# Gate tiles moved from the input projection into the scan, and a dt stage of its own, in a one-core decoder layer

## Chip, cores and metric

One core of one Trainium2 chip runs the whole layer as one program. The time is the device time of one execution in microseconds (us), as a median of runs: 3565.0 us over three runs, 3561.2 to 3567.3.

## The reference, cut to what matters

The layer is a selective scan block, a cross attention and a gated feed-forward, each followed by a layer norm. The change touches the first block, and the control flow of the second.

```
proj = hidden @ in_proj_w                  # 1024 x 1024 tokens by 1024 x 4096
x, z = split(proj)                         # x: 16 tiles of 128 channels, z: 16 gate tiles
xc = silu(conv4(x) + conv_b)
ssm = xc @ x_proj                          # 96 rows: 64 of dt, 16 of B, 16 of C
dt_r, Bm, Cm = rmsnorm of the three parts
dt = softplus(dt_r @ dt_proj + dt_bias)    # 16 tiles of 128 channels
scan over 512 steps, 16 states a channel:  h = exp(dt A) h + dt B xc ;  ys = C h
y = (ys + D * xc) * silu(z)
out = y @ out_proj                         # then residual and layer norm
```

Weights and activations are float32. The large products are made of three passes over pairs (high part, rest), at one pass a matmul; a product written directly on float32 operands shows as two matmul records.

## The kernel before, in words

Five phases run one after the other: `mamba_in`, `mamba_scan`, `project_norm_qkv`, `attention`, `attention_out_feed_forward`. A phase begins when every engine has ended the one before. Within a phase each engine has its own program in a fixed order, and semaphores tie them together; nothing is scheduled at run time.

`mamba_in` makes 32 tiles `main(m, s)` of 128 channels by 1024 tokens, each 8 x 2 x 3 = 48 matmuls (L95 to L97). Tiles 0 to 15 are x: VectorE convolves, ScalarE applies silu, and `xproj` adds the tile's share of the 96 rows. Tiles 16 to 31 are the gate z: ScalarE evicts each with Silu (L264) and SyncE stores it to `sz`. Once the 96 rows are whole, ScalarE and VectorE make their rms norm (L289 to L374), and the dt stage begins. It runs between the gate tiles, two dt tiles at a time: TensorE multiplies (L470), ScalarE makes |v|, relu(v), exp(-|v|) and ln(1 + exp) (L302, L303, L306, L311), VectorE a correction term and the sums (L382, L385, L389, L392), GpSimd the product u = dt * xc (L422; the last two are VectorE's, L406), and dt and u go to DRAM. xc stays in SBUF for the scan.

`mamba_scan` has 32 iterations (16 tiles of 128 channels, 2 batches) of 8 pairs of states. A pair n passes GpSimd (`dbx`, L725), ScalarE (exp into PSUM, L676), VectorE (the scan, L699, then the product with C, L688; for two pairs in eight the scan writes `g` itself and GpSimd multiplies, L713), and TensorE, which sums it over partitions. TensorE's program goes by t, two pairs each, 128 in all: at every fourth t the D term (L761), then `wait_product` and the four sums of t (L766), then two matmuls of the key projection of the context (`key_product`, L748). The pairs pass through four buffers `g`; pair n takes its buffer when the sums of pair n - 4 are done.

`project_norm_qkv` begins with 32 steps of the output projection. In each, SyncE loads y, the gate and the weights, GpSimd multiplies y by the gate (L1208), ScalarE and VectorE split into high part and rest, and TensorE multiplies. `attention` runs 32 heads in a loop of four rounds with eight heads each (`heads`, L1343).

Of the kernel before, what the change touches and what calls it, by code (L numbers as in the profile page):

```python
# [31 lines left out]
E = R + 2 * NS  # L32
CTX = 1024
# [66 lines left out]
def mamba_in(nc, res, d, xc):  # L100
# [21 lines left out]
    under = Arena(nc, "in_under", sb.at)  # L122
# [14 lines left out]
    dtw = [sb(f"dtw{s}", [R, P]) for s in range(2)]
    dt_b = sb("dt_b", [P, IT])

    ssm, sq, rms, ssm_n = acc[0][0:E], acc[1][0:E], pre[0][0:E], pre[1][0:E]  # L140
    rl, ee = ([over(f"{n}{s}", [P, B, L]) for s in range(2)] for n in ("rl", "ee"))
    dd, ll = acc, [pre[0], sb("ll", [P, B, L])]
# [8 lines left out]
    sz_st = [sem(f"sz_st{s}") for s in range(2)]  # L151
# [19 lines left out]
    sz, dt, u = (d[n].rearrange("(b i) p l -> i p b l", b=B) for n in ("sz", "dt", "u"))  # L171

    with nc.Block() as block:
        @block.sync
        def _(sp):
# [20 lines left out]
            sp.dma_start(dt_b[:], d["dt_bias"]).then_inc(par_ld, 16)  # L196
            for s in range(2):
                sp.dma_start(dtw[s][:], d["dt_w"][s]).then_inc(dtw_ld[s], 16)
            with sp.Fori(0, IT // 2) as j:
                for s in range(2):  # L200
                    next_w(2 * j + s, s)
            for s in range(2):
                next_w(IT + s, s)
                store_gate(IT + s, s)

            def store_dt(i, s):
                sp.wait_ge(dt_done, i + 1)
                sp.dma_start(dt[i], dd[s][:]).then_inc(dt_st[s], 16)

            def store_u(i, s):  # L210
                sp.wait_ge(u_done, i + 1)
                sp.dma_start(u[i], uu[s][:]).then_inc(u_st[s], 16)

            with sp.Fori(IT // 2 + 1, IT - 1) as j:
                next_w(2 * j, 0)
                store_gate(2 * j, 0)
                next_w(2 * j + 1, 1)
                i = 2 * j - IT - 2
                for s in range(2):
                    sp.wait_ge(dt_mm, i + s + 1)  # L220
                    sp.dma_start(dtw[s][:], d["dt_w"][i + s + 2]).then_inc(dtw_ld[s], 16)
                store_gate(2 * j + 1, 1)
                for s in range(2):
                    store_dt(i + s, s)
                for s in range(2):
                    store_u(i + s, s)
# [1903 lines left out]
```

## Time and profile before

| | |
|---|---|
| median of the runs | 3565.0 us (3561.2 to 3567.3) |
| the profiled execution | 3563.01 us, its span 3561.7 us |
| mamba_in, to the scan's first instruction | 0 to 432 us |
| mamba_scan, to its last store | 432 to 1235 us |
| project_norm_qkv | 1240 to about 1710 us |
| attention | about 1710 to 2405 us |
| busy over the span: TensorE, VectorE, ScalarE, GpSimd | 85%, 61%, 43%, 39% |

The shares are means over stages that have different limits: TensorE is at 9 tenths everywhere but in the scan, where VectorE is. Clock columns give the granted TensorE clock as a share of full speed; 0.50 is 1.2 GHz and 1.00 is 2.4 GHz. The durations of matmuls overlap, since matmuls are pipelined: the pace is read from their starts.

### The profile page before, as it was taken

How to read it: one execution, taken by the hardware profiler on the slowest of the kernel's cores; microseconds unless marked ns; L12 is line 12 of the kernel's file. 1: busy time of each engine (PE TensorE's matmuls, PEld its weight loads, DVE VectorE, ACT ScalarE, POOL GpSimd, SP SyncE). 2: the span in 40 equal slices, each digit the busy share in tenths (PEclk: the TensorE clock that was granted, in tenths of full speed). 3: DMA queues.
4: the chain of work that ended last, by engine and by line, in shares of the span. 5: the costliest groups of instructions: out<-in, count | busy, mean ns of one | idle time of the engine just before them, and what ended most of it. 6: DMA issues, size and time to landing. Idle time of an engine off the chain costs nothing. (4 is left out here: it accounts for less than half of the span.)

```text
span 3561.7 us, 39589 instructions
## 1 busy us (share of the span) xinstructions
PE 3035.0 (85%) x12955; PEld 2247.7 (63%) x12955; DVE 2181.1 (61%) x1669; ACT 1537.8 (43%) x2404; POOL 1395.1 (39%) x794
## 2 busy tenths in 40 slices
PE   9999745555555499999799999998799999999996
PEld 7877511111111178888587878776678888888884
DVE  6554489999999855701477777775644334324426
ACT  4457644554454432411387888772231121111111
POOL 0002299999999722000387878770100000000001
PEclk9999866666666699999899999998999999999998
DMA  3124474454454276312111111115311111111101
GB/s 111 41 77 168 165 180 109 112 118 109 113 119 110 73 281 205 128 66 92 63 37 32 31 36 31 31 33 200 94 52 45 44 56 53 35 53 53 47 18 59
DMA packets 150381, 310.04 MB, mean 87 GB/s; under 512 B 27488, under 2 KB 40544, under 8 KB 148864
## 3 DMA queue, kind: packets, MB, share of 16 engines
q1 hardware_dynamic: 132704, 299.13, 28.3%
q10 hardware_dynamic: 17568, 9.66, 0.9%
q8 instruction: 43, 0.70, 0.1%
q14 instruction: 66, 0.54, 0.1%
HBM read 244.45 MB, written 64.29 MB: 87 GB/s over the span
## 5 line engine op out<-in xcount | busy, mean ns | idle before, releaser
L725 POOL TENSOR_TENSOR scan_dbx<-scan_u,scan_b_bc 128x1024 f32<-128x1024 f32 x256 | 594.3, 2357 | 37.8 <-DMA scan_u<-u 37.8
L1512 POOL TENSOR_TENSOR at_p_lo<-at_p,at_p_hi 128x512 fp32r<-128x512 f32 x384 | 516.6, 1352 | 163.0 <-ACT at_p_hi L1418 152.8
L766 PE MATMUL scan_ps_y<-scan_g,scan_sel 128*32 128x512 f32 x1024 | 212.8, 914 | 355.1 <-DVE scan_g L688 330.9
L676 ACT ACTIVATE scan_ps_a<-scan_dt,scan_a_neg 128x512 f32<-128x512 f32 (+1 forms) x512 | 332.0, 680 | 380.4 <-DVE scan_g L688 365.2
L887 POOL TENSOR_TENSOR ff_y<-ff_y,ff_rstd 128x512 f32<-128x512 f32 x14 | 24.9, 1807 | 1123.3 <-DVE ff_rstd L876 1123.3
L699 DVE TENSOR_TENSOR_SCAN scan_ps_a<-scan_ps_a,scan_dbx 128x1024 f32<-128x1024 f32 x192 | 432.3, 2282 | 0.0
L1457 DVE TENSOR_REDUCE at_neg_max<-at_ps_mx 128x1 fp32r<-128x1536 f32 x132 | 232.0, 1758 | 168.8 <-PE at_ps_mx L1532 157.1
L766 PEld LDWEIGHTS scan_ps_y<-scan_g,scan_sel 128*32 128x32 f32 x1024 | 27.9, 129 | 473.0 <-DVE scan_g L688 291.6
L1415 ACT ACTIVATE at_p<-at_ps_s 128x512 f32<-128x512 f32 x384 | 227.8, 593 | 108.0 <-PE at_ps_s L1549 90.0
L1932 DVE TENSOR_TENSOR ff_hf<-ff_sg,ff_ps_u 128x1024 f32<-128x1024 f32 x28 | 34.2, 1221 | 388.3 <-PE ff_ps_u L97 388.3
L1418 ACT ACTIVATE at_p_hi<-at_p 128x512 fp32r<-128x512 f32 x384 | 242.8, 632 | 12.3
L688 DVE TENSOR_TENSOR scan_g<-scan_ps_a,scan_c_bc 128x1024 f32<-128x1024 f32 x192 | 230.4, 1200 | 0.3 <-PE scan_ps_y L766 0.3
L95 PE MATMUL in_ps<-in_x_hi,in_w_hi 128*128 128x512 f32 x512 | 202.5, 396 | 0.0
L96 PE MATMUL in_ps<-in_x_lo,in_w_hi 128*128 128x512 f32 x512 | 201.2, 393 | 0.0
L97 PE MATMUL in_ps<-in_x_hi,in_w_lo 128*128 128x512 f32 x512 | 200.7, 392 | 0.0
L748 PEld LDWEIGHTS scan_ps_x<-scan_cx,scan_wk 128*128 128x128 f32 x384 | 101.2, 291 | 155.2 <-issue 140.8
L95 PE MATMUL ff_ps_g<-ff_x_hi,ff_w_hi 128*128 128x512 f32 x448 | 176.2, 393 | 5.7 <-DVE ff_x_lo L1872 5.7
L748 PE MATMUL scan_ps_x<-scan_cx,scan_wk 128*128 128x256 f32 x384 | 174.0, 600 | 7.6 <-DMA scan_cx<-in_ctx 7.6
L96 PE MATMUL ff_ps_g<-ff_x_lo,ff_w_hi 128*128 128x512 f32 x448 | 175.2, 391 | 0.0
L97 PE MATMUL ff_ps_g<-ff_x_hi,ff_w_lo 128*128 128x512 f32 x448 | 174.9, 390 | 0.0
L95 PE MATMUL ff_ps_u<-ff_x_hi,ff_w_hi 128*128 128x512 f32 x448 | 174.7, 390 | 0.0
L97 PE MATMUL ff_ps_u<-ff_x_hi,ff_w_lo 128*128 128x512 f32 x448 | 174.3, 389 | 0.0
(254 smaller groups left out, 7429.6 us busy)
## 6 DMA issues: line engine op xcount, KB each, us to landing
scan_dt<-dt SPq DMA_DIRECT2D x128, 256.0 KB, 4.6
scan_u<-u SPq DMA_DIRECT2D x128, 256.0 KB, 7.6
ff_w<-in_w SPq DMA_DIRECT2D x56, 512.0 KB, 4.3
in_w<-in_w_in SPq DMA_DIRECT2D x32, 512.0 KB, 3.7
mid_w<-in_w_out SPq DMA_DIRECT2D x32, 512.0 KB, 5.0
ff_w<-in_w SPq DMA_DIRECT2D x56, 256.0 KB, 2.6
ff_wo_wo<-in_w_o SPq DMA_DIRECT2D x32, 384.0 KB, 3.0
sz<-in_xz SPq DMA_DIRECT2D x16, 512.0 KB, 3.0
```

The costliest lines, as they stand in the source:

```text
L95: nc.tensor.matmul(out, w_hi, x_hi, start=start, stop=False)
L96: nc.tensor.matmul(out, w_hi, x_lo, start=False, stop=False)
L97: return nc.tensor.matmul(out, w_lo, x_hi, start=False, stop=stop)
L676: nc.scalar.activation(at[:, h * L + h:(h + 1) * L], dt[it % 2][:, c, h:L], ACT.Exp, scale=a_neg[:, it % IT, e:e + 1]).then_inc(a_ready, 1)
L688: nc.vector.tensor_tensor(g[n % SG][:].rearrange("p (h l) -> p h l", h=2), ps_a[n % SA][:].rearrange("p (h l) -> p h l", h=2), c_bc[:, n / ...
L699: nc.vector.tensor_tensor_scan(out[:], ps_a[n % SA][:], dbx[n % SL][:], 0.0, ALU.mult, ALU.add).then_inc(scanned, 1)
L725: nc.gpsimd.tensor_tensor(dbx[n % SL][:].rearrange("p (h l) -> p h l", h=2), u[it % 2][:, c:c + 2], b_bc[:, b, k // 2].unsqueeze(1).to_bro ...
L748: last = nc.tensor.matmul(ps_x[:, 0:TOKS], wk[:, k, i * P:(i + 1) * P], cx[:, k], start=k == 0, stop=k == HT - 1)
L766: nc.tensor.matmul(ps_y[c * CW:(c + 1) * CW], sel[:], g[(2 * t + c // 2) % SG][:, h * L:(h + 1) * L], start=False, stop=m == NB - 1).then_ ...
L1418: nc.scalar.activation(p_hi[t % NSL][:], p[t % NSL][:], ACT.Copy).then_inc(p_hi_done, 1)
L1457: nc.vector.tensor_reduce(neg_max[:, i, HD:HD + 1], ps_mx[:].rearrange("p n l -> p (n l)"), AX_X, ALU.max, negate=True).then_inc(max_done, 1)
L1512: nc.gpsimd.tensor_tensor(p_lo[t % NSL][:], p[t % NSL][:], f32(p_hi[t % NSL][:]), ALU.subtract).then_inc(p_lo_done, 1)
```

## The change

Of the 16 gate tiles, `mamba_in` keeps two. The other 14 (`ZN`) are computed in the scan phase by TensorE, as plain float32 products, one tile and batch a unit of eight matmuls, in two halves of four. `UNITS` says at which of the 16 values of t in a block they stand; there are eight blocks, seven of them with four gate units each. The key projection goes the same way, a unit of eight matmuls at one t. For it the scan phase loads x, the weights `wz` and, since SBUF has no room left for xc, one tile of xc an iteration; `mamba_in` stores xc to DRAM. The gate is stored without silu, and the output projection applies it on ScalarE.

The dt stage now follows the last tile of `mamba_in`. It has four buffers each for exp, ln and dt, three PSUM slots for the product, a fourth PSUM tile for the correction term, no relu on ScalarE (VectorE takes the maximum with 0 and adds ln in one instruction), and dt_bias as a 65th row of the product. The loop of four rounds in `attention` is written out.

```diff
+ZN = IT - 2
 def mamba_in(nc, res, d):
-    NT = 2 * IT
+    NT = 2 * IT - ZN
+    ps_x, ps_t = [ps_dt[0], ps_dt[1], ps[0]], ps[1]
 # SyncE
+            def store_conv(m):
+                sp.wait_ge(xc_done, m + 1)
+                sp.dma_start(xc_out[m], xc4[:, :, m, :]).then_inc(xc_st, 16)
...
 # ScalarE
+            def exponentials(i):
+                act.wait_ge(dt_mm, i + 1)
+                if i >= ND:
+                    act.wait_ge(c_done, i - ND + 1)
+                nc.scalar.activation(ee[i % ND][:], ps_x[i % 3][:], ACT.Abs).then_inc(abs_done, 1)
+                act.wait_ge(abs_done, i + 1)
+                nc.scalar.activation(ee[i % ND][:], ee[i % ND][:], ACT.Exp, scale=-1.0).then_inc(e_done, 1)
+            def logarithm(i):
...
+            for i in range(0, IT, 2):
+                exponentials(i)
+                exponentials(i + 1)
+                logarithm(i)
+                logarithm(i + 1)
 # VectorE
+            for i in range(IT):
+                dve.wait_ge(e_done, i + 1)
+                dve.wait_ge(dt_done, i)
+                nc.vector.tensor_scalar(ps_t[:], ee[i % ND][:], 1.0, -1.0, ALU.add, ALU.add).then_inc(t_done, 1)
+                dve.wait_ge(l_done, i + 1)
...
+                nc.vector.scalar_tensor_tensor(dd[i % ND][:], ps_x[i % 3][:], 0.0, ll[i % ND][:],
+                                               ALU.max, ALU.add).then_inc(r_done, 1)
+                dve.wait_ge(t_done, i + 1)
+                nc.vector.tensor_tensor(ps_t[:], ee[i % ND][:], ps_t[:], ALU.subtract).then_inc(c_done, 1)
+                dve.wait_ge(c_done, i + 1)
+                dve.wait_ge(r_done, i + 1)
+                nc.vector.tensor_tensor(dd[i % ND][:], dd[i % ND][:], ps_t[:], ALU.add).then_inc(dt_done, 1)
 # TensorE
+            main(IT + 1, 1, mean_squares)          # the norm's two products stand in the middle of tile 17
+            def dt_product(i):
+                if i >= 3:
+                    pe.wait_ge(r_done, i - 2)
...
 def mamba_scan(nc, res, d):
-    KPB = 2
+    UNITS = {at: (kind, i) for i_at, (kind, i) in (
+        ((0, 2), ("z", 0)), ((2, 4), ("z", 1)), ((4, 5), ("k", 0)), ((6, 7), ("k", 1)),
+        ((8, 10), ("z", 2)), ((10, 12), ("z", 3)), ((12, 13), ("k", 2))) for at in range(*i_at)}
+    ENDS = {"z": (1, 3, 9, 11), "k": (4, 6, 12)}
...
+            def copy_gate(q):
+                m, b = divmod(q, B)
+                act.wait_ge(z_mm, q + 1)
+                act.wait_ge(z_st[b], 16 * m)
+                nc.scalar.activation(zb[b][:], ps_x[:], ACT.Copy).then_inc(zb_done, 1)
...
+            def gate_unit(q, half):
+                m, b = divmod(q, B)
+                if half == 0:
+                    pe.wait_ge(x_ld, 16 * HT)
+                    pe.wait_ge(wz_ld[m % ZC], 16 * (m // ZC + 1))
+                    free_x("z", q)
+                for k in range(HT // 2 * half, HT // 2 * (half + 1)):
+                    last = nc.tensor.matmul(ps_x[:], wz[m % ZC][:, k], x[:, k, b * L:(b + 1) * L], start=k == 0, stop=k == HT - 1)
...
 def project_norm_qkv(nc, res, d):
             def step(n, s):
+                act.wait_ge(a_ld[s], 32 * (n // 2 + 1))
+                nc.scalar.activation(gate[s][:], gate[s][:], ACT.Silu).then_inc(silu_done, 1)
                 act.wait_ge(used, n)
...
-                    pool.wait_ge(a_ld[s], 32 * (j + 1))
+                    pool.wait_ge(silu_done, 2 * j + s + 1)
 def attention(nc, res, d):
-        with eng.Fori(0, NW // 2) as j:
-            for s in range(2):
-                for g in range(G):
-                    body(2 * G * j + G * s + g, 2 * j + s, g, s)
+        for w in range(NW):
+            for g in range(G):
+                body(G * w + g, w, g, w % 2)
```

In VectorE's program of `mamba_in`, two dt tiles before read as follows (`over_ee` is exp, `pre` and `ll` are ln, `over_rl` is relu, `acc` is dt).

```order
L382 TENSOR_SCALAR in_acc_61<-in_over_ee_87 128x1024
L382 TENSOR_SCALAR in_acc_62<-in_over_ee_88 128x1024
L385 TENSOR_TENSOR in_acc_61<-in_over_ee_87,in_acc_61 128x1024
L385 TENSOR_TENSOR in_acc_62<-in_over_ee_88,in_acc_62 128x1024
L389 TENSOR_TENSOR in_acc_61<-in_acc_61,in_pre_63 128x1024
L389 TENSOR_TENSOR in_acc_62<-in_acc_62,in_ll 128x1024
L392 TENSOR_TENSOR in_acc_61<-in_acc_61,in_over_rl_85 128x1024
L392 TENSOR_TENSOR in_acc_62<-in_acc_62,in_over_rl_86 128x1024
```

Now two dt tiles of VectorE are these (`in_ps` is the PSUM tile of the correction term, `in_ps_dt` the product).

```order
L349 TENSOR_SCALAR in_ps<-in_tail_ee_81 128x1024
L354 SCALAR_TENSOR_TENSOR in_tail_dd_89<-in_ps_dt,in_tail_ll_85 128x1024
L357 TENSOR_TENSOR in_ps<-in_tail_ee_81,in_ps 128x1024
L360 TENSOR_TENSOR in_tail_dd_89<-in_tail_dd_89,in_ps 128x1024
L349 TENSOR_SCALAR in_ps<-in_tail_ee_82 128x1024
L354 SCALAR_TENSOR_TENSOR in_tail_dd_90<-in_ps_dt,in_tail_ll_86 128x1024
L357 TENSOR_TENSOR in_ps<-in_tail_ee_82,in_ps 128x1024
L360 TENSOR_TENSOR in_tail_dd_90<-in_tail_dd_90,in_ps 128x1024
```

It is four instructions a tile in both, but one tile after the other in place of two interleaved, and each has at most one SBUF operand beside a PSUM one.

TensorE's program in the scan, from its start, was this (`scan_g` are the pairs, `scan_ps_x` the key projection).

```order
L761 MATMUL scan_ps_y<-xc,scan_d_diag_1466 32x512 x4
L766 MATMUL scan_ps_y<-scan_g_1455,scan_sel 32x512 x2
L766 MATMUL scan_ps_y<-scan_g_1456,scan_sel 32x512 x2
L748 MATMUL scan_ps_x<-scan_cx,scan_wk 128x256 x2
L766 MATMUL scan_ps_y<-scan_g_1457,scan_sel 32x512 x2
L766 MATMUL scan_ps_y<-scan_g_1458,scan_sel 32x512 x2
L748 MATMUL scan_ps_x<-scan_cx,scan_wk 128x256 x2
```

It is now this.

```order
L786 MATMUL scan_ps_y<-scan_xs_1334,scan_d_diag_1328 32x512 x4
L792 MATMUL scan_ps_y<-scan_g_1317,scan_sel 32x512 x2
L792 MATMUL scan_ps_y<-scan_g_1318,scan_sel 32x512 x2
L772 MATMUL scan_ps_x<-scan_x,scan_wz_1337 128x512 x4
L792 MATMUL scan_ps_y<-scan_g_1319,scan_sel 32x512 x2
L792 MATMUL scan_ps_y<-scan_g_1320,scan_sel 32x512 x2
L772 MATMUL scan_ps_x<-scan_x,scan_wz_1337 128x512 x4
```

Four matmuls of 512 columns stand where two of 256 did, and the first of them, at t = 0, needs all of `scan_x`.

SyncE's issues at the start of the scan phase went, after u of iteration 1, straight to the key weights (`scan_wk`) and the context.

```order
L577 DMA scan_c_bc<-bc 32x2048 x4
L571 DMA scan_dt_1448<-dt 32x4x512 x4
L571 DMA scan_u_1450<-u 32x4x512 x4
L598 DMA scan_wk<-in_w_k 128x3072
L590 DMA scan_cx<-in_ctx 128x8x256
```

Ten loads of 512 KB (x and the first two `wz`) and two of 256 KB (xc) now come before them.

```order
L548 DMA scan_c_bc<-bc 32x2048 x4
L561 DMA scan_xs_1334<-xc 128x512
L542 DMA scan_dt_1310<-dt 32x4x512 x4
L542 DMA scan_u_1312<-u 32x4x512 x4
L561 DMA scan_xs_1335<-xc 128x512
L583 DMA scan_x<-in_x_t 128x1024 x8
L564 DMA scan_wz_1337<-in_w_in 128x1024
L564 DMA scan_wz_1338<-in_w_in 128x1024
L586 DMA scan_wk<-in_w_k 128x3072
L572 DMA scan_cx<-in_ctx 128x8x256
```

## Rows read from the trace of the kernel before

**Rows 1.** Busy tenths in 40 slices of the span (the page).
```profile
PE   9999745555555499999799999998799999999996
DVE  6554489999999855701477777775644334324426
```
**Rows 2.** Two stretches: length, busy us (count) by engine, clock, DMA share, GB/s.
```profile
218.00:420.00 202.00, 200.32 (x794) 148.97 (x793) 93.19 (x77) 143.88 (x133) 43.97 (x14) 0.98 0.42 148
463.00:1232.00 769.00, 425.31 (x1648) 134.90 (x1648) 767.32 (x444) 380.97 (x841) 730.64 (x315) 0.66 0.48 113
```
**Rows 3.** Order of time in mamba_in: start, us, engine, line, operation, idle before.
```profile
218.52 1.03 ACT L264 ACTIVATE in_xz<-in_ps 128x1024 f32<-128x1024 f32 x1 [2.69 <-PE in_ps L97]
219.91 1.02 ACT L289 ACTIVATE in_acc<-in_ps_dt 96x1024 f32<-96x1024 f32 x1 [0.35 <-PE in_ps_dt L97]
418.00 0.39 PE L95 MATMUL in_ps<-in_x_hi,in_w_hi 128*128 128x512 f32 x1
419.37 0.39 PE L95 MATMUL in_ps<-in_x_hi,in_w_hi 128*128 128x512 f32 x1
427.40 1.25 SPq L242 DMA_DIRECT2D bc<-in_pre  x1
432.22 0.41 ACTq L648 DMA_DIRECT2D scan_a_exp<-in_a_log  x1
```
**Rows 4.** Groups of instructions in 0 to 450 us: busy us, mean ns.
```profile
L470 PE MATMUL in_ps_dt<-in_pre,in_dtw 64*128 64x512 f32 x64 | 30.5, 618 | 1.7 <-DMA in_dtw<-in_dt_w 1.7
L372 DVE RECIPROCAL in_acc<-in_pre 96x1024 f32<-96x1024 f32 x1 | 6.5, 6550 | 9.8 <-ACT in_pre L294 9.8
L363 DVE SCALAR_TENSOR_TENSOR in_pre<-in_xz,in_cw,in_acc 128x1024 f32<-128x1024 f32 x32 | 41.1, 1285 | 4.4
L382 DVE TENSOR_SCALAR in_acc<-in_over_ee 128x1024 f32<-128x1024 f32 x16 | 11.1, 695 | 45.0 <-ACT in_over_ee L306 44.8
L302 ACT ACTIVATE in_over_ee<-in_ps_dt,in_dt_b 128x1024 f32<-128x1024 f32 x16 | 17.8, 1111 | 2.9 <-DVE in_acc L392 2.9
L306 ACT ACT_TABLE_LOAD x8 | 10.3, 1283 | 0.1
```
**Rows 5.** GpSimd's u product and VectorE beside it, in order of time.
```profile
313.35 6.40 POOL L422 TENSOR_TENSOR in_under_uu<-in_acc,xc 128x1024 f32<-128x1024 f32 x2 [19.86 <-DVE in_acc L392]
314.69 2.80 DVE L332 TENSOR_TENSOR in_w_lo<-in_w,in_w_hi 128x1024 fp32r<-128x1024 f32 x1 [0.53 <-ACT in_w_hi L254]
```
**Rows 6.** One round of the scan, in order of time.
```profile
702.83 2.08 PE L748 MATMUL scan_ps_x<-scan_cx,scan_wk 128*128 128x256 f32 x4
706.47 1.06 PE L766 MATMUL scan_ps_y<-scan_g,scan_sel 128*32 128x512 f32 x8
707.46 1.13 PE L748 MATMUL scan_ps_x<-scan_cx,scan_wk 128*128 128x256 f32 x4
708.43 1.20 DVE L688 TENSOR_TENSOR scan_g<-scan_ps_a,scan_c_bc 128x1024 f32<-128x1024 f32 x1
709.56 2.27 DVE L699 TENSOR_TENSOR_SCAN scan_g<-scan_ps_a,scan_dbx 128x1024 f32<-128x1024 f32 x1
713.09 1.93 PE L766 MATMUL scan_ps_y<-scan_g,scan_sel 128*32 128x512 f32 x8 [4.50 <-DVE scan_g L688]
718.59 0.64 PE L766 MATMUL scan_ps_y<-scan_g,scan_sel 128*32 128x512 f32 x4 [1.96 <-DVE scan_g L688]
```
**Rows 7.** Stretches of 2 us: TensorE busy (count), clock, DMA share, GB/s.
```profile
704.00:706.00 2.00, 2.00 (x11) 0.53 0.34 131
706.00:708.00 2.00, 1.92 (x15) 1.00 0.21 70
```
**Rows 8.** Start of the scan phase: a 10 us stretch, and TensorE's first key product.
```profile
450.00:460.00 10.00, 0.00 (x0) 0.00 (x0) 6.21 (x3) 1.39 (x3) 8.59 (x4) 0.50 1.03 216
472.55 2.05 PE L748 MATMUL scan_ps_x<-scan_cx,scan_wk 128*128 128x256 f32 x4 [7.61 <-DMA scan_cx<-in_ctx]
```
**Rows 9.** TensorE's waits in attention, 1740 to 2405 us: total, times, longest.
```profile
PE at_ps_s L1547 <- ACT at_p L1415: 7.3, 3, 3.2
```

More of the change, by code:

```diff
@@ L131, in mamba_in @@
     zero = sb("zero", [P, P], F32R)
-    uu = [under(f"uu{s}", [P, B, L]) for s in range(2)]
-    assert under.at <= sb.at
-    over = Arena(nc, "in_over", sb.at)
     xc_hi = [sb(f"xc_hi{s}", [P, B, L], F32R) for s in range(2)]
     xc_lo = [sb(f"xc_lo{s}", [P, B, L], F32R) for s in range(2)]
[L137 to L142, printed above, removed]
+    ssm, sq, rms = acc[0][0:E], acc[1][0:E], pre[0][0:E]
+    bcn, dtr = acc[0][R:E], pre[1][0:R + 1]
+    tail = Arena(nc, "in_tail")
+    ee, ll, dd = ([tail(f"{n}{s}", [P, B, L]) for s in range(ND)] for n in ("ee", "ll", "dd"))
+    uu = [tail(f"uu{s}", [P, B, L]) for s in range(2)]
+    assert tail.at <= BASE + 8 * HT * TOK
     assert sb.at <= TOP - 4 * B * IT * L
@@ L210, in store_u @@
-            def store_u(i, s):
+                sp.dma_start(dt[i], dd[i % ND][:]).then_inc(dt_st[i % ND], 16)
                 sp.wait_ge(u_done, i + 1)
[L212 to L226, printed above, removed]
@@ L248, in _ @@
                 sp.wait_ge(u_st[s], 16 * IT // 2)
+            for s in range(ND):
+                sp.wait_ge(dt_st[s], 16 * IT // ND)
         @block.scalar
@@ L430, in main @@
                     pe.wait_ge(x_lo_done, k + 1)
+                    if between is not None and k == HT // 2:
+                        between()
                     for b in range(B):
@@ L558, in pool_pairs, with units, unit_end @@
         return sum(by_pool(i) for i in range(n))
-    def unit_end(q):
-        c, i = divmod(q, KF)
-        return BPC * c + (HT * (i + 1) - 1) // KPB
+    def units(c, kind):
+        per = len(ENDS[kind])
+        return range(per * c, min(per * (c + 1), {"z": B * ZN, "k": KF * NCH}[kind]))
+    def unit_end(kind, q):
+        c, i = divmod(q, len(ENDS[kind]))
+        return BPC * c + ENDS[kind][i]
     with nc.Block() as block:
@@ L595, in _ @@
             load_rows(c_bc, 0, NS, c_ld[0])
+            load_xs(0)
             load_dt(1)
             load_u(1)
+            load_xs(1)
+            for k in range(HT):
+                sp.dma_start(x[:, k], d["x_t"][k]).then_inc(x_ld, 16)
+            for m in range(ZC):
+                load_wz(m)
             sp.dma_start(wk[:], d["w_k"]).then_inc(wk_ld, 16)
@@ L609, in _ @@
                     load_u(it + 2)
+                    sp.wait_ge(xs_done, it + 1)
+                    load_xs(it + 2)
+                for q in range(B * ZN):
+                    if (unit_end("z", q) + 4) // NB == it:
+                        store_z(q)
+                        if q % B == B - 1 and q // B + ZC < ZN:
+                            load_wz(q // B + ZC)
                 c, last = divmod(it + 1, NIT // NCH)
@@ L2066, in phase @@
         res.release()
-    phase(mamba_in, d, xc)
-    phase(mamba_scan, d, xc)
+    phase(mamba_in, d)
+    phase(mamba_scan, d)
     phase(project_norm_qkv, d)
```

270 lines of the change are left out of this document (120 added, 150 removed).

## The prediction, made before the changed kernel was run

> **What bounds the kernel now.** I read the page's slices first, then the two stretches, the order of time at the seams between phases, and the waits. TensorE stands at 9 tenths nearly everywhere except from slice 5 to 13, the scan, where it stands at 4 or 5 and VectorE at 9 [rows 1]. In the part of mamba_in that makes gate tiles, TensorE is busy 200.3 of 202 us, VectorE 93 [rows 2]: that part lasts as long as its products. In the scan VectorE is busy 767.3 of 769 us and TensorE 425 at a mean clock of 0.66 [rows 2]: that part lasts as long as VectorE's instructions, and TensorE has 344 us of gaps. So the change takes work from a stretch that TensorE sets and puts it where it doesn't set the time. What matters is what is left in mamba_in, whether the gaps are wide enough one by one, and what the new work waits for.
>
> **mamba_in.** Up to the end of tile 16, whose eviction starts at 218.5 us [rows 3], nothing on the path changes. The stores of xc (512 KB, one for each tile of about 13 us) stand on SyncE ahead of a weight load that was due a whole tile before its use, so I cost them at nothing; without that cover each load could be late by the convolution's time, up to half a tile or 5.5 us.
>
> Before, 15 more tiles followed, and the next phase began at 432.2 [rows 3]. Now comes one tile and then the dt stage, bare. Its start on this time axis: the rms part begins at 219.9 [rows 3]; half of tile 17 is 24 matmuls by 0.228 us (six starts in 1.37 us, rows 3), 5.5, so 225.4; the norm's two products are 4 records by 0.48 (30.5 us over 64 in rows 4, the nearest float32 group), 227.3; the root some 1.7, 229.0; the reciprocal 6.55 [rows 4], 235.6; the scaling 1.3, 236.9. The rest of tile 17 is done by then (233). The first dt product takes 1.9, 238.8. ScalarE then needs |v|, table, exp, |v|, exp, table, ln: five by 1.1 and two table loads by 1.28 [rows 4], 8.1, 246.9. Three VectorE instructions finish tile 0: 250.7.
>
> From there each tile costs VectorE four instructions. One SCALAR_TENSOR_TENSOR is 1.285 [rows 4]. A product that reads PSUM took 1.20 [rows 6], I take it for the two subtractions and sums. The TENSOR_SCALAR took 0.695 from SBUF to SBUF [rows 4]; now it writes PSUM, which no row shows. Below it can stay 0.70, above it goes at the rate of the others, 1.20. I take 1.20, since all rows with a PSUM operand are there. With 0.1 for two starts that wait for the result just before, a tile is 5.0 us.
>
> On that one instruction a rule of the Trainium skill (VectorE: DVE Perf Modes, "Why PSUM operands drop a tier") speaks against the change: any PSUM operand takes away the doubled rate of float32. By that rule the cost is 1.2, without it 0.7, and the stage would be 6 us shorter.
>
> ScalarE's floor per pair is six by 1.1 plus two tables, 9.2, so 4.6 a tile, just under. TensorE's is 1.9 at 2.4 GHz, 3.8 at 1.2 GHz, under as well. 15 tiles by 5.0 are 75: 325.7. GpSimd's last product is 3.2 (6.40 for two, rows 5), 328.9. From the last store's issue to the next phase took 4.8 (427.4 to 432.2, rows 3): 333.7. Gain 432.2 - 333.7 = 98.5 us.
>
> The doubt is the period. GpSimd makes a u product beside every tile. Where it ran before, VectorE's subtraction of two SBUF operands beside it took 2.80 instead of about 1.2 [rows 5]. In the scan, where GpSimd is busy 730.6 of 769 us [rows 2], the product with a PSUM operand took 1.20 [rows 6]. The new stage has at most one SBUF operand an instruction, so I take no loss; if one instruction a tile is held like the one in rows 5, it is 6.6 us a tile, and 24 us are lost. Bounds: 4.6 and 6.6, that is 6 us better to 24 us worse.
>
> The Trainium skill (SBUF — State Buffer, "SBUF: two separate sides") has the pair of ports that VectorE shares with GpSimd as an exclusive lock, taken by Vector instructions with two SBUF inputs. The trace agrees with 2.80 against 1.20, and by that rule the new stage is free of it.
>
> **Start of the scan.** TensorE's first unit, at t = 0, waits for all of x and wz. Before, its first key product waited for the context until 472.55, the idle time 7.6 us [rows 8], behind 2.6 MB of key weights and context. Now 5.8 MB (ten loads of 512 KB, two of 256 KB) must land in their place, 3.2 MB more, with the DMA engines full already (share 1.03 at 216 GB/s, rows 8). At 216 GB/s that is 14.6 us later. TensorE is in order, so the sums of t = 1 stand behind the first half unit (5.5 us, between its times at the two clocks below, since it starts at 1.2 GHz). They end some 18 us later than before, and pair 6 can't have its buffer. Before, the sums of t = 1 came just in time, so VectorE stands still for most of it. I take 13 us. Below: x comes in long rows and may load faster, 6; above 20.
>
> **Units in the scan.** At 2.4 GHz four key records of 256 columns took 1.13, at 1.2 GHz 2.08 [rows 6]. The difference, 0.95, is what their 1024 columns take at full clock, and 0.18 is left as fixed. A half gate unit is eight records of 512, 4096 columns: 4.0 and 7.8 us. The sums take 1.06 and 1.93 [rows 6]. The sums start at 706.47, 713.09 and 718.59, so 6.6 and 5.5 us apart by turns [rows 6]. A step at full clock is 1.06 + 4.0 = 5.1, with the D term (as long as the sums) 6.1: it fits, the last one 0.6 late where 5.5 are to be had. How late may the sums of an even t be? Those that start at 706.47 free the buffer that the scan at 709.56 writes, so they may come 3.09 - 1.06 = 2.0 us late. At half clock a step is 9.7 and does not fit; but then TensorE has no gap at all, and after being busy all through 704 to 706 its clock went to 1.00 [rows 7]. So I expect the clock to be at 2.4 GHz in all steps but the first of each run of units, and a delay now and then: 5 us in all. Below 0, above 25 (14 runs of units by 1.8).
>
> ScalarE gets 28 evictions of about 0.6 us, but is busy 381 of 769 [rows 2]; its wait for the end of a unit comes no later than its wait for VectorE, at full clock. DMA goes up by about 22 MB (gate out, weights, xc in), 29 GB/s on 113 at share 0.48 [rows 2]: hidden.
>
> **Output projection and attention.** Silu on ScalarE lies ahead of each step, with TensorE the bound (24 matmuls by 0.228, 5.5 us a step) and ScalarE at 2.3 a step: I take 1 us for the first step, and 0 to 4 as its bounds. In attention, TensorE waited three times for ScalarE, 7.3 us in total [rows 9], once at each return of the loop. The loop is gone, and TensorE is the bound there, so 7.3 us are gained; below that 0, if the long straight code brings waits of its own. What comes late next there is nothing regular: the rest of the stage is busy.
>
> **Sum.** 3563.0 (the profiled execution) - 98.5 + 13 + 5 + 1 - 7.3 = 3476.2. That execution is 2.0 below the median of 3565.0, so I forecast 3478 us.
>
> **Rivals.**
> A. The dt stage is slower than 5.0 us a tile, by GpSimd's reading or by ScalarE and VectorE taking turns. For it speaks that no row shows the stage alone, against it rows 6. At 6.6 a tile: 3478 + 24 = 3502.
> B. TensorE comes late at most unit steps, since the clock falls in the gaps of steps 5, 7 and 13 to 15 and each run starts at half rate, or a half unit is longer than 4.0. If every one of the 56 half units costs 1 us of VectorE's time: 3478 - 5 + 56 = 3529. For it: the mean clock of 0.66 [rows 2]; against it: the 2.0 us of slack, and that these steps leave few gaps.
> C. Slower than before: the clock stays at 1.2 GHz through the units, and TensorE sets the scan. A run of five steps then takes 5 by 9.7 and two D terms of 1.9, 52.3, in place of 5 by 6.06, 30.3; less 2.0 of slack it is 20 late. Fourteen such runs: 280 us, so 3478 - 5 + 280 = 3753. It decides the sign once a run costs over 6 us. For it: half of the scan runs at that clock now; against it rows 7.
> D. The change doesn't do what it says, in that the gate products only move the bound: TensorE's gaps are filled, but the loads at the start and in the loop delay u and dt of the next iterations. Each iteration late by 1 us: 3510.
>
> **How the numbers follow.** Forecast 0.66, A 0.12, B 0.08, D 0.06, C 0.05, others 0.03. The forecast's own range is 3478 with 24 below (6 + 7 + 5 + 1, and 5 for smaller things) and about 30 above; A and D lie in or near it, B at its edge. The range 3454 to 3530 leaves out C and a part of the rest. A measurement of this kernel can tell 0.2%, about 7 us, from no change. Faster by more than that: all but C and half of the others, 0.92; within it 0.02; slower 0.06.
>
> **What would show it.** The scan phase's first instruction at 334 instead of 432 us; the four VectorE instructions of the dt stage at 1.2 to 1.3 each and a period of 5.0; a wait of TensorE's first gate product for x until about 487 - 98 = 389, with VectorE waiting behind it; half units of 4.0 us and a mean clock in the scan well above 0.66; VectorE still at full share in the scan after the start; no idle 3 us gap on TensorE in attention. The forecast is wrong if VectorE waits for the sums (scan_ps_y) by tens of us, or if the dt stage takes over 6 us a tile.

## The result and the profile after

The changed kernel takes 3465.5 us (median of 4 runs, 3463.6 to 3470.2), the kernel before in the same comparison 3563.1 us: ratio 0.9726, 95% interval 0.9711 to 0.9741. The forecast was 3478 us, range 3454 to 3530. The profiled execution took 3465.8 us, its span 3464.5 us, at a mean granted clock of 0.917 (0.899 before).

The page's slices of the profile after, each a fortieth of the span:

```profile
PE   8994567776774799998999999979899999999996
DVE  5557799999999565401777777764734324324326
```

Against [rows 1], VectorE stands at 9 in slices 6 to 13, where it did in 7 to 13, and TensorE beside it stands mostly at 6 and 7 instead of 4 and 5. By stretches (length, busy us and count of PE, PEld, DVE, ACT, POOL, clock, DMA share, GB/s), the dt stage and the scan:

```profile
218.00:333.00 115.00, 75.39 (x130) 30.77 (x128) 85.96 (x69) 75.44 (x70) 37.60 (x16) 0.58 0.46 171
363.00:1132.00 769.00, 526.36 (x2052) 195.94 (x2048) 750.05 (x433) 390.29 (x854) 722.62 (x312) 0.80 0.58 148
```

Beside [rows 2]: in 769 us of scan TensorE does 101 us more, and VectorE 17 us less; two waits at the start (12.7 us) and eight small ones (7.0 us), all shown below, are more than that. The phases, from first instruction to first instruction, read from the order of time:

| phase | before | after | difference | forecast |
|---|---|---|---|---|
| mamba_in | 432.22 | 331.45 | -100.8 | -98.5 |
| scan | 807.65 | 825.85 | +18.2 | 13 + 5 |
| output projection | 476.1 | 476.3 | +0.2 | +1 |
| attention | 696.5 | 681.95 | -14.6 | -7.3 |
| feed forward | 1149.2 | 1148.9 | -0.3 | 0 |

**The dt stage.** In order of time (start, us, engine, line, instruction, idle before), the norm's reciprocal, one tile, and the end of the phase:

```profile
229.38 6.55 DVE L340 RECIPROCAL in_acc<-in_pre 96x1024 f32<-96x1024 f32 x1 [9.67 <-ACT in_pre L271]
...
315.93 2.35 POOL L376 TENSOR_TENSOR in_tail_uu<-in_tail_dd,xc 128x1024 f32<-128x1024 f32 x1 [2.50 <-DVE in_tail_dd L360]
315.96 1.23 DVE L349 TENSOR_SCALAR in_ps<-in_tail_ee 128x1024 f32<-128x1024 f32 x1
317.09 1.22 DVE L354 SCALAR_TENSOR_TENSOR in_tail_dd<-in_ps,in_tail_ll 128x1024 f32<-128x1024 f32 x1
318.22 1.22 DVE L357 TENSOR_TENSOR in_ps<-in_tail_ee,in_ps 128x1024 f32<-128x1024 f32 x1
319.48 1.22 DVE L360 TENSOR_TENSOR in_tail_dd<-in_tail_dd,in_ps 128x1024 f32<-128x1024 f32 x1
...
327.99 0.36 SPq L221 DMA_DIRECT2D u<-in_tail_uu  x1
331.45 0.41 ACTq L651 DMA_DIRECT2D scan_a_exp<-in_a_log  x1
```

The next tile's TENSOR_SCALAR starts at 320.80: a period of 4.85 us (315.96 to 320.80), VectorE without a gap. TENSOR_SCALAR into PSUM takes 1.23 us, where [rows 4] had 0.695 into SBUF. GpSimd's product is 2.35 us, not the 3.2 worked out from [rows 5]. At the stage's start, after an idle 3.83 us, TensorE's granted clock is 0.50, and the first tile's product (L427) takes 3.8 us, from 237.50 until ScalarE begins on it at 241.29.

**The start of the scan:**

```profile
376.85 5.20 PE L772 MATMUL scan_ps_x<-scan_x,scan_wz 128*128 128x512 f32 x8 [13.51 <-DMA scan_wz<-in_w_in]
381.98 1.06 PE L792 MATMUL scan_ps_y<-scan_g,scan_sel 128*32 128x512 f32 x8
382.98 3.70 PE L772 MATMUL scan_ps_x<-scan_x,scan_wz 128*128 128x512 f32 x8
383.26 1.23 DVE L694 TENSOR_TENSOR scan_g<-scan_ps_a,scan_c_bc 128x1024 f32<-128x1024 f32 x1 [8.45 <-PE scan_ps_y L792]
386.76 0.60 ACT L636 ACTIVATE scan_zb<-scan_ps_x 128x512 f32<-128x512 f32 x1 [16.91 <-issue]
388.73 2.29 DVE L705 TENSOR_TENSOR_SCAN scan_g<-scan_ps_a,scan_dbx 128x1024 f32<-128x1024 f32 x1 [4.24 <-ACT scan_ps_a L684]
```

VectorE's 8.45 us are a wait for the sums (L792), which stand on TensorE behind the first half unit (L772), and that one behind a gate weight. The 4.24 us are a wait for ScalarE: it reached the eviction of the first gate tile (L636), waited there 16.91 us for the tile, and the decays (the exp into PSUM) behind it in its queue were late. After that all of VectorE's waits up to the end of the scan are these (engine, line, waited for: us, times, longest), 0.3 to 1.3 us each. The kernel before has no wait of VectorE for ScalarE in the scan.

```profile
DVE scan_ps_a L705 <- ACT scan_ps_a L684: 7.0, 8, 1.3
```

What such a wait stands behind, in one place near the end of the scan:

```profile
1134.15 5.46 PE L761 MATMUL scan_ps_x<-scan_cx,scan_wk 128*128 128x256 f32 x16
1139.64 0.38 ACT L627 ACTIVATE scan_kb<-scan_ps_x 128x256 f32<-128x256 f32 x1 [2.76 <-PE scan_ps_x L761]
1140.43 1.30 ACT L682 ACTIVATE scan_ps_a<-scan_dt,scan_a_neg 128x512 f32<-128x512 f32 x2 [0.40 <-ACT scan_kb L627]
1141.92 2.30 DVE L705 TENSOR_TENSOR_SCAN scan_ps_a<-scan_ps_a,scan_dbx 128x1024 f32<-128x1024 f32 x1 [0.95 <-ACT scan_ps_a L684]
```

A key unit is now whole in one step, and here, after a gap, it is 5.46 us long; between gate units, at the full clock, it is 3.72 (at 398.78). ScalarE stands at its eviction for 2.76 us, and VectorE gets its decays 0.95 us late.

**Attention.** The three waits of [rows 9] are gone, and 14.6 us with them. What came behind one of them in the kernel before, in order of time, and then stretches of 2 us (as above: length, PE, PEld, DVE, ACT, POOL, and then the clock):

```profile
1914.00 0.66 PE L1547 MATMUL at_ps_s<-at_q_hi,at_k_hi 97*128 97x512 f32 x1 [3.15 <-ACT at_p L1415]
1914.46 0.63 PE L1548 MATMUL at_ps_s<-at_q_lo,at_k_hi 96*128 96x512 f32 x1
1914.88 0.63 PE L1549 MATMUL at_ps_s<-at_q_hi,at_k_lo 96*128 96x512 f32 x1
```
```profile
1914.00:1916.00 2.00, 2.00 (x5) 1.61 (x6) 0.00 (x0) 1.97 (x4) 1.31 (x2) 0.55 0.00 0
1916.00:1918.00 2.00, 2.00 (x7) 1.53 (x7) 0.05 (x1) 0.87 (x2) 2.00 (x2) 0.60 0.01 4
1918.00:1920.00 2.00, 2.00 (x10) 1.64 (x9) 1.97 (x2) 1.23 (x2) 0.45 (x1) 1.00 0.00 0
```

A matmul of 0.40 us before the gap takes 0.63 behind it, and for some 4 us TensorE gets through 5 and 7 in 2 us where 10 is its rate after. From one head's start to the next it is 24.9, 23.7 and 24.0 us across the three returns, and 19.9 at the same place without a return: 12.9 us more in all, of which the waits are 7.3.

### The profile page after: what moved, and what is told of

Its sections match the earlier page's. It is cut to its first block and busy times, and to the rows that moved or that the text cites. A ratio compares the mean times of both kernels' runs of the same rounds, so it can differ in the third digit from the quotient of the medians.

```text
span 3464.5 us, 37038 instructions
## 1 busy us (share of the span) xinstructions
PE 3015.0 (87%) x12731; PEld 2191.7 (63%) x12731; DVE 2160.8 (62%) x1655; ACT 1502.2 (43%) x2400; POOL 1391.3 (40%) x796
## 3 DMA queue, kind: packets, MB, share of 16 engines
q8 instruction: 62, 1.02, 0.1%
## 5 line engine op out<-in xcount | busy, mean ns | idle before, releaser
L918 POOL TENSOR_TENSOR ff_y<-ff_y,ff_rstd 128x512 f32<-128x512 f32 x14 | 24.9, 1806 | 1123.0 <-DVE ff_rstd L907 1123.0
L792 PE MATMUL scan_ps_y<-scan_g,scan_sel 128*32 128x512 f32 x1024 | 176.2, 765 | 220.8 <-DVE scan_g L694 216.3
L772 PE MATMUL scan_ps_x<-scan_x,scan_wz 128*128 128x512 f32 x448 | 230.0, 661 | 13.5 <-DMA scan_wz<-in_w_in 13.5
L792 PEld LDWEIGHTS scan_ps_y<-scan_g,scan_sel 128*32 128x32 f32 x1024 | 25.2, 119 | 334.1 <-issue 175.1
L772 PEld LDWEIGHTS scan_ps_x<-scan_x,scan_wz 128*128 128x128 f32 x448 | 89.5, 211 | 164.7 <-issue 164.7
L98 PE MATMUL ff_ps_y<-ff_h_hi,ff_w_lo 128*128 128x512 f32 x448 | 174.3, 389 | 0.0
L97 PE MATMUL ff_ps_u<-ff_x_lo,ff_w_hi 128*128 128x512 f32 x448 | 174.3, 389 | 0.0
L97 PE MATMUL ff_ps_y<-ff_h_lo,ff_w_hi 128*128 128x512 f32 x448 | 174.3, 389 | 0.0
```

The costliest lines, as they stand in the source:

```text
L97: nc.tensor.matmul(out, w_hi, x_lo, start=False, stop=False)
L98: return nc.tensor.matmul(out, w_lo, x_hi, start=False, stop=stop)
L772: last = nc.tensor.matmul(ps_x[:], wz[m % ZC][:, k], x[:, k, b * L:(b + 1) * L], start=k == 0, stop=k == HT - 1)
```

## The experiments

| run | us, median | ratio to before | 95% interval |
|---|---|---|---|
| e1_unroll_only | 3552.5 | 0.9964 | 0.9951 to 0.9978 |
| changed kernel | 3465.5 | 0.9726 | 0.9711 to 0.9741 |
| e2_gates_later | 3452.6 | 0.9682 | 0.9669 to 0.9696 |
| e3_term_in_sbuf | 3491.9 | 0.9796 | 0.9783 to 0.9810 |
| e4_gate_quarter | 3464.8 | 0.9711 | 0.9698 to 0.9725 |
| e5_keys_later | 3456.8 | 0.9694 | 0.9681 to 0.9707 |
| e6_term_reordered | 3473.1 | 0.9738 | 0.9724 to 0.9751 |
| e7_gate_double | 3606.4 | 1.0112 | 1.0097 to 1.0128 |
| e8_three_edits | 3450.9 | 0.9674 | 0.9661 to 0.9687 |
| e9_gates_and_keys | 3443.2 | 0.9655 | 0.9642 to 0.9668 |
| e10_gpsimd_copy | 3470.9 | 0.9729 | 0.9714 to 0.9744 |

The kernel before gave 3563.1, 3565.6, 3567.4 and 3567.3 us in the four comparisons. So differences between medians of two comparisons carry some 4 us of doubt, and I lean on phase times and waits of the profiles where they are that small.

**The loop in attention alone**, on the kernel before.

```
-        with eng.Fori(0, NW // 2) as j:
-            for s in range(2):
-                for g in range(G):
-                    body(2 * G * j + G * s + g, 2 * j + s, g, s)
+        for w in range(NW):
+            for g in range(G):
+                body(G * w + g, w, g, w % 2)
```

> The kernel before with the one edit that attention's loop over the sequence windows is written out. In the two traces attention lost 14.6 us, where the prediction counted 7.3 (three waits at the loop's returns). Theory: a return costs more than its wait, since the matmuls behind the gap run at a lower granted clock; read by the spacing of the heads (24.91, 23.67 and 23.96 us across a return, against 19.9 for any other) the three returns hold 12.9 us, and with the entry some 14 us: 3549 us, and head spacings of 19.9 at the three places. Rival: the loop holds only its waits, and the other 7 us come from the scan's or the projection's new timing in the changed kernel: 3556 us, with part of the spacings staying at 21 to 22.

3552.5 against 3565.6 us, 13.1 less (interval 8 to 17). The head spacing at the three returns is now 19.9 us each time, and none of the others but the first (22.4, before 22.5) is over 20.4. The theory holds: the loop held about 13 us, and the 7.3 of its waits are below the interval. The rival's 3556 us would be within it; the spacings decide against it.

**The gate tiles one block later**, on the changed kernel. Block c computes what block c - 1 did, and SyncE issues x and the first gate weights behind the rows of batch 1.

```
-            for k in range(HT):
-                sp.dma_start(x[:, k], d["x_t"][k]).then_inc(x_ld, 16)
-            for m in range(ZC):
-                load_wz(m)
...
+                if it == 0:
+                    for k in range(HT):
+                        sp.dma_start(x[:, k], d["x_t"][k]).then_inc(x_ld, 16)
+                    for m in range(ZC):
+                        load_wz(m)
...
-                    q = len(ENDS[kind]) * c + i
+                    q = len(ENDS[kind]) * (c - ZB[kind]) + i
```

> The changed kernel with its gate tiles one block later: blocks 1 to 7 of the scan hold them and not 0 to 6, and SyncE issues the loads of x and of the first gate weights behind the rows of the second batch, not ahead of the scan's first rows. Theory: the 12.7 us that VectorE waits at the scan's start (8.45 and 4.24 us) come from the first gate weight, which lands at 376.9 us and holds TensorE's queue, and ScalarE's behind it, in front of the scan's own products; one block later they have landed, and the time is 3465.5 - 12.7 = 3453 us, with no wait of VectorE over 2 us in the first block. Rival: what is late is the scan's own dt and u rows, because so many loads stand in the queues, or the wait is only moved to the second block, whose loads then meet the next batch's rows: 3462 to 3470 us.

3452.6 us, as the theory said. The scan phase falls from 825.9 to 813.6 us, and of VectorE's waits for ScalarE and TensorE in it only 6.4 us in seven pieces are left. The late u and dt rows of the rival are not seen.

**The correction term in SBUF**, on the changed kernel.

```
-                nc.vector.tensor_scalar(ps_t[:], ee[i % ND][:], 1.0, -1.0, ...)
+                nc.vector.tensor_scalar(ts[:], ee[i % ND][:], 1.0, -1.0, ...)
```

> The changed kernel with the correction term of the dt stage in an SBUF tile in place of the PSUM bank. The TENSOR_SCALAR is then SBUF to SBUF (0.70 us in the kernel before, 1.23 into PSUM in the changed one), and the subtraction of the term has two SBUF operands. Theory of a lock between VectorE and GpSimd: instructions of VectorE with two SBUF operands and GpSimd's u product (2.35 us a tile now, 3.16 in the kernel before, where such instructions ran beside it) hold each other up. If GpSimd's product goes back to 3.2 us and VectorE's three two-operand instructions are lengthened, the period grows from 4.85 us to between 5.2 and 6.6 us a tile: +5 to +28 us over 16 tiles, centrally +20, 3485 us. Rival without a lock: the period falls by 0.53 us to 4.3 or 4.45 us: -6 to -8 us, 3458 us.

3491.9 us, 26 more: near the upper bound of what the theory of a lock gave. In order of time, one tile of this run:

```profile
277.65 2.34 POOL L377 TENSOR_TENSOR in_tail_uu<-in_tail_dd,xc 128x1024 f32<-128x1024 f32 x1 [4.15 <-DVE in_tail_dd L361]
277.68 2.86 DVE L350 TENSOR_SCALAR in_tail_ts<-in_tail_ee 128x1024 f32<-128x1024 f32 x1
280.47 1.21 DVE L355 SCALAR_TENSOR_TENSOR in_tail_dd<-in_ps,in_tail_ll 128x1024 f32<-128x1024 f32 x1
281.60 1.21 DVE L358 TENSOR_TENSOR in_tail_ts<-in_tail_ee,in_tail_ts 128x1024 f32<-128x1024 f32 x1
282.84 1.22 DVE L361 TENSOR_TENSOR in_tail_dd<-in_tail_dd,in_tail_ts 128x1024 f32<-128x1024 f32 x1
```

GpSimd starts 0.03 us ahead and isn't lengthened, 2.34 us. The TENSOR_SCALAR, which with GpSimd idle took 0.69 us at its first tile, ends 0.55 us behind GpSimd's end. The period is 6.49 us, 1.64 more; over the 15 tiles that stand beside a product of GpSimd that is 25 us, and `mamba_in` is 23.5 us longer. My expectation had the parts wrong: I counted GpSimd's product at 3.2 us and the two-operand instructions as lengthened. Here those don't meet GpSimd at all, and the one that does, with a single SBUF operand and an SBUF result, bears the whole.

**A quarter of the gate's products**, on the changed kernel. The expectation speaks of four groups of six matmuls; it is four matmuls, two records each.

```
-                for k in range(HT // 2 * half, HT // 2 * (half + 1)):
+                for k in ((0,), (HT - 1,))[half]:
```

> The changed kernel with one of the four groups of six matmuls left in each half unit of the gate tiles (so the gate's sums are incomplete), loads, evictions and stores as they were. It prices the matmuls of the gate inside the scan. Theory of the forecast: they lie in time that TensorE had spare, and take 5 us at most from the scan beyond its start; 4 to 8 us go, 3460 us. Rival B of the prediction: each half unit makes the next step's sums late by about 1 us, so that most of 56 half units are worth 1 us: 3410 to 3420 us. Rival of the clock: with fewer columns TensorE's granted clock falls below the 0.80 that the scan has now, the scan's own products at the lower clock come late, and the time rises by more than 2 us.

3464.8 us: no difference clear of the doubt, so rival B is off by 45 to 55 us, and the gain of 4 to 8 us that the forecast's theory gave doesn't show. The scan phase took 824.8 us (825.9). The granted clock between 363 and 1132 us fell from 0.80 to 0.67, as the third expected, but the time did not rise. At the start VectorE waited 8.7 us for the first unit and its eviction, in place of 12.7; against that its waits for GpSimd were 2.3 us longer. Its small waits for ScalarE stayed, 7.6 us in seven: they aren't from the gate's products.

**The keys' eviction one pair later**, on the changed kernel.

```
-                    if n == 2 * unit_end("k", q) + 6:
+                    if n == 2 * unit_end("k", q) + 7:
                         store_keys(q)
```

> The changed kernel with ScalarE's eviction of each key unit one pair of states later (about 3 us). In the changed kernel VectorE waits eight times, 0.3 to 1.3 us each and 7.0 us in all, for the decays of ScalarE; the kernel before has no such wait. Behind the four waits looked at stands the eviction of a key unit whose 16 matmuls ran at the half clock (5.46 us, and ScalarE waited 2.76 us for it). Theory: ScalarE's order is the cause of what the scan lost beyond its start; with the eviction one pair later it never waits that long, VectorE's waits go, and the time is 3465.5 - 7 = 3459 us. Rival: TensorE is what is late, and whoever evicts later only moves the wait to the next unit or to the sums: 3464 to 3468 us.

3456.8 us. The small waits are gone from the list, and the scan phase is 820.1 us, 5.7 less, with 1.3 us more at its start (9.7 for 8.45). So about 7 of the 18.2 us came from this place of the eviction in ScalarE's order. The median's difference, 8.7 us, agrees with that within the doubt.

**The term in SBUF, moved away from GpSimd's product**, on the changed kernel: the next tile's TENSOR_SCALAR is issued between the subtraction and the last addition.

```
                 nc.vector.tensor_tensor(ts[i % 2][:], ee[i % ND][:], ts[i % 2][:], ALU.subtract)...
+                if i + 1 < IT:
+                    term(i + 1)
```

> The changed kernel with the correction term in two SBUF tiles and the TENSOR_SCALAR of the next tile issued ahead of the last addition of this one, so that it no longer stands beside GpSimd's u product (2.35 us from the end of that addition; the sum max(x,0)+log and the subtraction, 1.21 us each, stand beside it now). With the term in SBUF and the old order the TENSOR_SCALAR took 2.86 us and ended 0.55 us behind GpSimd's product, and the time rose by 26 us. Theory: only this one instruction, a single SBUF operand and an SBUF result, is held by GpSimd's; away from it it takes 0.70 us, and the period is 0.70 + 3 x 1.21 = 4.35 us in place of 4.85: 3457 us. Rival: instructions with two SBUF operands lengthen GpSimd's product (3.16 us in the kernel before), the subtraction now beside it does so, and the TENSOR_SCALAR is held till its end: a period of about 5.2 us, 3471 us.

3473.1 us, 7.6 more: near the rival's time. The period is 5.24 us for 4.85, 5.5 us from the first product of GpSimd to the last; the rest is within the doubt. One tile:

```profile
276.70 1.21 DVE L359 SCALAR_TENSOR_TENSOR in_tail_dd<-in_ps_dt,in_tail_ll 128x1024 f32<-128x1024 f32 x1
276.86 2.35 POOL L383 TENSOR_TENSOR in_tail_uu<-in_tail_dd,xc 128x1024 f32<-128x1024 f32 x1 [2.90 <-DVE in_tail_dd L367]
277.83 2.45 DVE L362 TENSOR_TENSOR in_tail_ts<-in_tail_ee,in_tail_ts 128x1024 f32<-128x1024 f32 x1
280.21 0.68 DVE L351 TENSOR_SCALAR in_tail_ts<-in_tail_ee 128x1024 f32<-128x1024 f32 x1
280.81 1.21 DVE L367 TENSOR_TENSOR in_tail_dd<-in_tail_dd,in_tail_ts 128x1024 f32<-128x1024 f32 x1
```

The TENSOR_SCALAR is now at 0.68 us, and the subtraction of two SBUF operands is the one that is held: 2.45 for 1.21 us, ending 1.07 us behind GpSimd's end at 279.21. The rival had the time and not the mechanism: GpSimd's product is not lengthened, VectorE's instruction is. The SCALAR_TENSOR_TENSOR with its PSUM operand runs beside GpSimd at 1.21 us.

In the runs with the term in SBUF, GpSimd started first wherever the two met. The kernel before shows the other order. At 391.61 VectorE begins three instructions with two SBUF operands, 1.2 us each as when alone, and ends them at 395.10; GpSimd begins two products at 393.15 and takes 6.57 us. Two products of 2.35 behind the 1.95 us until VectorE's end are 6.65. So there GpSimd is the one that waits. The same reading gives the 6.40 us of [rows 5]: VectorE's last sum ran until 314.16, 0.8 us into the first product, and the subtraction (L332), itself held, until 317.49, 1.05 us into the second; with twice 2.35 that is 6.55. So the 3.2 us taken for a product holds waits of its own.

**Any instruction of GpSimd?** The term in SBUF in the old order, GpSimd's product replaced by a copy.

```
-                nc.gpsimd.tensor_tensor(uu[i % 2][:], dd[i % ND][:], xc4[:, :, i, :], ALU.mult)...
+                nc.gpsimd.tensor_copy(uu[i % 2][:], dd[i % ND][:])...
```

> The changed kernel with the correction term in SBUF in the old order (3492 us), and GpSimd's u product replaced by a copy of dt, so that it has one operand in SBUF where it had two (u is then dt, and the scan's values are other ones). In the run before, VectorE's TENSOR_SCALAR was held to the end of GpSimd's product: 2.86 us for 0.69. If any instruction of GpSimd holds it, it now ends about 0.6 us behind the copy's end, and the period is 6.5 us less what the copy is shorter than 2.35 us. If only GpSimd's two operands do, it takes 0.69 us and the period is 0.70 + 3 x 1.21 = 4.35 us: 35 us less than 3492, some 3457 us.

```profile
277.38 1.04 POOL L377 COPY in_tail_uu<-in_tail_dd 128x1024 f32<-128x1024 f32 x1 [4.13 <-DVE in_tail_dd L361]
277.43 1.54 DVE L350 TENSOR_SCALAR in_tail_ts<-in_tail_ee 128x1024 f32<-128x1024 f32 x1
```

3470.9 us, and the TENSOR_SCALAR again ends 0.55 us behind GpSimd's end (278.97 and 278.42). The hold lasts as long as GpSimd's instruction, and one SBUF operand of GpSimd holds this instruction as two do.

The Trainium skill (SBUF — State Buffer, "SBUF: two separate sides") has a pair of ports that VectorE and GpSimd share: whichever starts first has it for a whole instruction, either GpSimd's or one of VectorE's in a two-port mode or with two SBUF inputs (the latter only against a GpSimd instruction that reads SBUF), and "the other fully blocks". The three runs agree: held with two inputs (2.45 us for 1.21), held in what I take for the two-port mode, since it goes at 0.69 us where others need 1.21 (2.86 us), free with a PSUM operand (1.21 us). What is held ends behind GpSimd by its own time less 0.14 us in each case (0.55 of 0.69, 1.07 of 1.21). An instruction at the slower rate with one SBUF operand and no PSUM operand was not tried.

**Twice the gate's products in each half unit**, on the changed kernel.

```
-                for k in range(HT // 2 * half, HT // 2 * (half + 1)):
+                for k in ((0, 1, 2, 3, 1, 1, 1, 1), (6, 6, 6, 6, 4, 5, 6, 7))[half]:
```

> The changed kernel with eight matmuls in place of four in each half unit of the gate tiles (the added ones repeat a group of the sum, so the gate's values are other ones). A quarter of the work left the time where it was; this asks from where on TensorE's gate work decides. A half unit is then 7.4 us at the full clock, with the sums (1.06 us) and every fourth step the product with d (1.07 us) 8.7 us in a step of 6.1 us: 2.6 us late at each, 10.4 us at the end of each of the two rows of four in a block, over 7 blocks. If VectorE's buffers give 2.0 us of slack, as the prediction took: 14 x 8.4 = +118 us, 3583 us. If they give 8 us: 14 x 2.4 = +34 us, 3500 us. If TensorE's time were no bound even so, the time would stay within 5 us.

3606.4 us, 141 more and 1.1% slower than the kernel before. The two largest of VectorE's waits in the scan (engine, line, waited for: us, times, longest), and ScalarE's eviction of a gate tile ahead of one of them:

```profile
DVE scan_g L705 <- ACT scan_ps_a L684: 76.2, 14, 7.7
DVE scan_g L705 <- PE scan_ps_y L792: 51.1, 14, 4.0
```
```profile
746.16 0.60 ACT L636 ACTIVATE scan_zb<-scan_ps_x 128x512 f32<-128x512 f32 x1 [9.54 <-issue]
```

Both come 14 times, once in each row of four half units: 9.1 us a row, where slack 2.0 gave 8.4 and slack 8 gave 2.4. A half unit is 7.1 us and not 7.4, and the first of a row ran at the lower clock, 8.76; with these the expectation's sum is 9.3 + 1.7 - 2.0 = 9.0. So a step must hold the unit: 3.70 us fits, 7.1 doesn't. The sum fits a slack of 2.0, but it doesn't show it: more than half of the waits are for decays of ScalarE, which stands 9.54 us at the gate's eviction until the late unit is done, and only 51.1 us are for the sums that the slack was worked out for.

**Three edits at once:** e2, e5 and e6.

> The changed kernel with three edits at once: the gate tiles one block later (measured alone: 13 us less), the keys' eviction one pair later and the reordered dt stage (both measured beside this run). They touch three places that don't overlap in time, so by the theories they add: 3465.5 - 13 - 7 - 8 = 3437.5 us. If both rivals of the last two hold: 3452 + 6 = 3458 us.

3450.9 us. The expected 3437.5 had the reordered dt stage as a gain of 8 us, and it cost 7.6. With the measured terms, 3465.5 - 12.9 - 8.7 + 7.6 is 3451.5: they add.

**The two that pay.**

> The changed kernel with the two edits that paid by themselves: gate tiles one block later (13 us less) and the keys' eviction one pair later (9 us less), the dt stage as in the changed kernel. If they add, as the run of three edits suggests (3451 us with a dt stage that costs 8 us more): 3465.5 - 13 - 9 = 3443.5 us, and no wait of VectorE over 1 us between the scan's first pair and its end. If they overlap (the keys' gain came partly from the first block): 3446 to 3450 us.

3443.2 us (3442.9 to 3447.1), ratio 0.9655 (0.9642 to 0.9668), the fastest of all. VectorE's waits between 325 and 1140 us, all of them:

```profile
DVE scan_g L708 <- POOL scan_dbx L734: 28.1, 2, 27.9
```

That is the start of the phase, which the kernel before has too (28.9). The scan phase is 806.3 us, against 807.65 before with no gate tile in it.

## Why the prediction was right, point by point

- **What bounds each stretch:** right. TensorE's work in the scan is free as long as each step holds it: with a quarter of the gate's products the time stayed, with twice as many it rose by 141 us.
- **mamba_in, -98.5 us:** measured -100.8. The period was 4.85 us for 5.0 (2.3 us over 15 tiles): the SCALAR_TENSOR_TENSOR was 1.22 and not 1.285, and the 0.1 for two waits isn't there, the four starts being 1.13 to 1.32 us apart. GpSimd's last product took 2.35 for 3.2, the end 3.5 us (327.99 to 331.45) for 4.8. Against that, the first tile ended 2.1 us later (252.8 for 250.7). The step that failed in it is "the first dt product takes 1.9": TensorE had been idle for 3.83 us and took 3.8 at the lower clock. The eviction of tile 16 was also 1.15 us later than in [rows 3], at 219.67, but a shorter root (1.11 for 1.7) and other small terms made up for that. The undecided price, TENSOR_SCALAR into PSUM, is 1.23, as taken. No run moved the gate tiles with the old dt stage, so the 100.8 us aren't split between the two.
- **No loss beside GpSimd:** right, and for the reason given, but the reason was told too narrowly. "At most one SBUF operand an instruction" doesn't protect: the TENSOR_SCALAR with its result in SBUF has one and was held, for some 25 us in all. No instruction with a PSUM operand was held in any of these runs (1.21 to 1.23 us beside GpSimd), and each of the stage's instructions has one. Whether the TENSOR_SCALAR into PSUM is free because of the operand itself or because it has lost its fast form, the runs don't separate.
- **Start of the scan, +13 us:** 12.7 measured, by two errors that cancel. The step "3.2 MB more, at 216 GB/s that is 14.6 us later" failed: the gate weight landed at 376.9 and not 389, some 5 us later than the context did in the kernel before (472.55 less 100.8 is 371.8). The loads came faster than the 216 GB/s of [rows 8]: 361 between 361 and 371 us and 422 between 371 and 377, when x and the weights were due. And the prediction counted only TensorE's queue. 5.1 us of landing and 3.15 of a longer first unit (5.20 for 2.05) make 8.25 of the 8.45; the other 4.24 are ScalarE's queue, standing at the gate's eviction. That the two errors left the sum at 12.7 is luck.
- **Units in the scan, +5 us:** 5.5 measured, by another cause. That a step holds a half unit was right (3.70 us for 4.0), and so the gate's products cost nothing that shows after the start. Whether the slack is 2.0 us stays open. What cost was a key unit, whole in one step at the lower clock, with its eviction in ScalarE's order ahead of decays. "Its wait for the end of a unit comes no later than its wait for VectorE, at full clock" was the sentence, and the clock is where it failed. Moving the eviction took the waits away, 7.0 us. The 5.5 are these less 1.5 us of other differences, of which the largest is a shorter wait of VectorE for GpSimd at the phase's start (26.8 for 28.9 us).
- **Attention, -7.3 us: the mis-sized term.** 14.6 measured, 13.1 with the loop alone. I counted the waits of [rows 9] and nothing behind them. After such a gap on the engine that sets the time, the matmuls took 0.63 us each for 0.40, for about 4 us: over the three returns that is 5.6 us beside the 7.3 of waits.
- **Rivals:** A, B, C and D did not come. A's price of 24 us is about what the term in SBUF costs, 26. One part of C's mechanism, TensorE setting the scan, is what twice the products brings.
- **Sum:** 12.5 us under the forecast: 7.3 from attention, 2.3 from mamba_in, 0.8 from the projection, 0.3 from the last phase, less 0.2 in the scan. The other 2.0 are the base, which the forecast raised to the median shown (3565.0), while the kernel before took 3563.1 in the comparison.

## What to carry to other kernels

Here work moved into the gaps of an engine was free where it fitted step by step, and its cost was in the other queues that it entered. So place its loads where nothing waits behind them, and its evictions late enough for the unit's time at the lower clock; these two were worth 22 us after the change. Price a stall of the engine that sets the time with the slower instructions behind it, not by its wait alone. Beside a busy GpSimd, look at every VectorE instruction for a PSUM operand. Count one without it as held until GpSimd's instruction ends, if GpSimd started first and it has two SBUF inputs or runs in the fast form (the TENSOR_SCALAR's 0.69 us).

## What the runs showed of the hardware

- VectorE's TENSOR_SCALAR of 128x1024 float32 from SBUF to SBUF: 0.69 us alone, 2.86 beside GpSimd's product of 2.34 (e3), 1.54 beside its copy of 1.04 (e10); into PSUM 1.23, beside GpSimd or not (the changed kernel).
- A subtraction of two SBUF operands: 1.21 us alone (e3), 2.45 when GpSimd's product had begun 0.97 us earlier (e6). GpSimd's time was 2.34 to 2.35 in both. Where VectorE started first, in the kernel before, GpSimd's two products took 6.57 us.
- In the scan phase's start the DMA moved 212 to 236 GB/s while rows of dt, u and bc came, and 422 GB/s while x and gate weights were due, the share of the engines being 1.02 to 1.05 in both. Whether the shape of the rows is the cause wasn't tried.
- A half gate unit of eight records of 512 columns: 3.70 us at 2.4 GHz.
